# Flamingo-style gated decoder, layer 1 attention: the finishing of a unit is issued between the maxima and the scores of its batch

## The reference, cut to what matters

```python
xn = (x - mu) * jax.lax.rsqrt(var + EPS) * ln_g + ln_b
q = _split_heads(xn @ Wq)
kv = xn @ Wkv
k = _split_heads(kv[..., :INNER])
v = _split_heads(kv[..., INNER:])
mem = _split_heads(memories @ Wm)
k = jnp.concatenate([k, mem], axis=2)
v = jnp.concatenate([v, mem], axis=2)
scale = DIM_HEAD ** (-0.5)
dots = jnp.einsum('bhid,bhjd->bhij', q, k) * scale
attn = jax.nn.softmax(dots, axis=-1)
out = jnp.einsum('bhij,bhjd->bhid', attn, v)
...
return out @ Wo + bo
```

## Time and profile before

| | us |
|---|---|
| median of 3 runs | 5704.32 |
| lowest and highest | 5701.73, 5706.47 |
| profiled execution | 5706.84 |
| its span (first to last instruction of the program) | 5705.1 |
| units of layer 1 attention in it | about 442 to 2883 |

### The profile page before, as it was taken

One profiled execution on the slowest core, in us unless ns is written; L12 is line 12 of the kernel. 1 busy time (PEld: TensorE's weight loads), 2 busy tenths in 40 slices (PEclk: granted clock), 3 DMA queues, 4 the chain that ended last, 5 costly groups with the idle time before them and its releaser, 6 DMA issues. The chain is left out here.

```text
span 5705.1 us, 74603 instructions
## 1 busy us (share of the span) xinstructions
PE 5058.3 (89%) x26863; PEld 1958.8 (34%) x26872; DVE 4773.0 (84%) x5111; ACT 3066.1 (54%) x5929; POOL 1556.1 (27%) x1168
## 2 busy tenths in 40 slices
PE   8939999999999999999932799999997599999997
PEld 5524444445454544444411222222223122222222
DVE  7459989898989899899868899999982799999993
ACT  3314444444444444444410288888882188888884
POOL 0015556565656565655612000000000200000000
PEclk9969999999999999999965799999995599999996
DMA  0043233333324232322102211111100411111100
GB/s 30 1 131 101 65 94 86 91 87 85 104 67 122 55 115 53 105 70 55 28 4 61 47 21 21 26 21 21 26 7 7 100 21 21 25 22 21 21 16 5
DMA packets 164054, 293.78 MB, mean 51 GB/s; under 512 B 26492, under 2 KB 103752, under 8 KB 160616
## 3 DMA queue, kind: packets, MB, share of 16 engines
q1 hardware_dynamic: 159592, 287.70, 20.4%
q10 hardware_dynamic: 4096, 1.29, 0.1%
HBM read 178.92 MB, written 109.89 MB: 51 GB/s over the span
## 5 line engine op out<-in xcount | busy, mean ns | idle before, releaser
L1599 DVE TENSOR_REDUCE a_mx<-ps 128x1 f32<-128x1024 f32 x1536 | 1820.2, 1220 | 151.4 <-PE ps L1479 129.4
L1566 ACT ACTIVATE a_prob<-ps 128x512 f32<-128x512 f32 (+1 forms) x3264 | 1705.3, 601 | 426.9 <-PE ps L1467 422.2
L1060 ACT ACTIVATE prob<-ps 128x512 f32<-128x512 f32 (+1 forms) x1888 | 975.0, 602 | 1181.9 <-PE ps L945 1181.8
L1163 POOL TENSOR_TENSOR tot_p<-tot_p,prob 128x512 f32<-128x512 f32 (+1 forms) x896 | 1340.4, 1496 | 921.6 <-ACT prob L1060 856.6
L1088 DVE TENSOR_REDUCE mx<-ps 128x1 f32<-128x1024 f32 x896 | 1051.3, 1215 | 152.9 <-PE ps L922 145.1
L1111 DVE TENSOR_TENSOR tot_d<-tot_d,prob 128x512 f32<-128x512 f32 x928 | 1047.8, 1129 | 87.6 <-ACT prob L1060 36.2
L1479 PE MATMUL ps<-a_K,a_Q 51*128 51x512 bf16 (+1 forms) x3328 | 1068.3, 385 | 49.6 <-DMA a_Q<-q_stack_dram 30.3
L1467 PE MATMUL ps<-a_Q,a_K 51*128 51x512 bf16 (+1 forms) x3264 | 1003.8, 389 | 82.8 <-ACT a_prob L1566 76.6
L1503 PE MATMUL ps<-a_prob,a_V 128*9 128x512 f32 x6528 | 953.9, 609 | 10.9 <-ACT a_acc L1550 10.9
L956 PE MATMUL ps<-prob,V 128*64 128x512 f32 (+1 forms) x3776 | 934.0, 605 | 0.0
L944 PE MATMUL ps<-QA,KA 128*128 128x512 f32 (+1 forms) x1888 | 806.4, 427 | 0.0
(11 more groups left out here) (348 smaller groups left out, 3243.4 us busy)
## 6 DMA issues: line engine op xcount, KB each, us to landing
a_K<-k_stack_dram SPq DMA_DIRECT2D x64, 600.4 KB, 5.8
k_hi_dram<-hi_s SPq DMA_DIRECT2D x112, 256.0 KB, 2.0
k_lo_dram<-lo_s SPq DMA_DIRECT2D x112, 256.0 KB, 2.0
KA<-k_hi_dram SPq DMA_DIRECT2D x64, 384.0 KB, 4.3
KA<-k_lo_dram SPq DMA_DIRECT2D x64, 384.0 KB, 5.5
KB<-k_hi_dram SPq DMA_DIRECT2D x64, 384.0 KB, 6.5
k_bf_dram<-bf_s SPq DMA_DIRECT2D x112, 128.0 KB, 1.7
KM<-k_bf_dram SPq DMA_DIRECT2D x32, 448.0 KB, 7.1
```

The costliest lines, as they stand in the source:

```text
L1060: nc.scalar.activation(prob[0:r, batch % 2, t % BATCH, :], c.banks(n % 3)[0:r, :], ACT.Exp, scale=SCALE).then_inc(exped, 1)
L1163: nc.gpsimd.tensor_tensor(tot_p[0:r, u % 2, :], tot_p[0:r, u % 2, :], p, ALU.add).then_inc(totalled_p, 1)
L1566: nc.scalar.activation(prob[0:r, batch % 2, t % BATCH, :], c.banks(n % 3)[0:r, :], ACT.Exp, scale=SCALE).then_inc(exped, 1)
L1599: nc.vector.tensor_reduce(mx[:, u % 2, j, i % FULL:i % FULL + 1], c.banks(slot(step), 2), AX.X, ALU.max).then_inc(maxed, 1)
```

## The change

In the loop over the batches the finishing is issued earlier on two engines. On PE it now stands between the maxima and the scores of batch 1; before, it stood between the scores and the weighing. On DVE it now stands between the two reductions of maxima and the two row sums of batch 1; before, it stood behind the row sums. The numbers of the slots, the waits, the instructions themselves, and the order on ACT, POOL and SP are the same. It applies to 31 of the 32 finishings; the one behind the last batch stays where it is.

```diff
@@ PE
                         for step in max_steps(u, b):
                             max_score(*step)
+                        kind, what = extra_of(u, b) or (None, None)
+                        if kind == "fin":
+                            finish(what)
                         for t in tiles_of(b):
                             score(u, t)
-                        kind, what = extra_of(u, b) or (None, None)
                         if kind == "k":
                             project(what)
                         if kind == "v":
                             project_v(*what)
-                        if kind == "fin":
-                            finish(what)
```

## The result

The changed kernel takes 5779.76 us (median of 4, 5772.55 to 5788.25) against 5703.49 before: a ratio of 1.013, 95% interval 1.0117 to 1.0143. It is 76 us slower. The forecast was slower as well, but by 48 us, and its range ended at 5770. The profiled execution took 5779.97 us, with a span of 5777.1.

The account below looks back on a forecast made before the run. The prediction took PE to set the pace, with DVE trailing and PE stopping only at finishings. Order +20.6 us and clock +27 us, about 48 in all, on 5704.3 gave 5752 us, range 5719 to 5770.

Parts of the forecast that it names:

- What bounds the kernel: Layer 1's units: PE sets the pace and stops only at finishings, 23 times, 28.4 us in all, waiting for DVE.
- DVE's lag costs nothing: Time from PE's first maximum of batch 1 to DVE's start on it, 0.44 to 1.32 us, had not cost PE anything.
- DVE is the bound after all: Rival: DVE's queue delays the units, so the 28.4 us of stops are gained and the new wait covered; 5676 us, chance 0.03.
- DVE's lag shrinks: Rival: DVE reaches batch 1 only 0.43 us behind PE in all units, clock up; 5712 us, chance 0.05.
- The stop removed, the stop added: On PE: 28.4 us at batch 2's second maximum go; the finishing waits for its batch's first reduction, about 46 us in all.
- The order's cost: PE's new order without any clock effect, summed over three kinds of unit and unit 31: +20.6 us.
- The number of falls: PE's granted clock drops at three of four of the new stops: 23 falls, bounds 0 and 30.
- The last finishing of the kernel before: Sign: behind the last batch PE idles 0.88 us, then runs the finishing, and the granted clock falls to 0.55.
- What one fall costs: PE's clock lowered for 3.4 us, read from layer 0: 1.2 us lost, bounds 0 and 1.54; +27 us in all.
- its dearest case: Rival: PE's clock falls at every place and at full price, 20.6 + 46 = 67 us; 5771 us, chance 0.07.
- the clock holds: Rival: PE's clock stays up at the new stops, so only +20.6 us counts; 5725 us, chance 0.23.

Follow-up runs that it names:

- DVE's half alone: Kernel before with only DVE's finishing moved ahead of its two row sums, PE's order unchanged: 5695.51 us, ratio 0.998.
- the kernel with the stop filled: Changed kernel plus six score matmuls that do no useful work ahead of each finishing on PE: 5726.55 us, ratio 1.0036.
- PE's half alone: Kernel before with only PE's finishing moved between maxima and scores, DVE's order unchanged: 5785.1 us, ratio 1.0142.
- the kernel with the wait apart: Changed kernel with PE's wait kept between maxima and scores, the finishing's matmuls put back behind the scores: 5781.87 us; run again, 5756.74 us.
- the version with the split row sums: Kernel before with DVE's finishing moved between its two row sums of batch 1, PE's order unchanged: 5672.63 us, ratio 0.9944.

## Why the prediction was wrong, point by point

**What bounds the kernel.** Right on PE and on the stops. The claim that DVE's lag costs nothing was true of the kernel before and held in the changed one, but it had less room than I gave it: in the kernel with DVE's half alone, 1.26 us of idle time on DVE was enough to give back 23 of 34 us. The rival "DVE is the bound after all" was therefore wrong about this change and half right about the kernel. DVE's row sums did get shorter, 0.69 us each in unit 2 in place of 3.38 for both, and PE had no use for that time. "DVE's lag shrinks" did not come true: in unit 2 it stayed at 0.80, and in unit 3 it went only from 1.32 to 1.09.

**The stop removed, the stop added.** Right. 28.4 us gone, 47.1 added at 30 places (forecast about 46), up to 2.0 us long (2.1). The order's cost came out at 17.5 us against 20.6, and the kernel with the stop filled lies 20.5 us above the kernel before. Each kind was 0.05 to 0.2 us cheaper than its sum, partly because the reduction releases its slot a little earlier than 1.36 us after its start (1.31 to 1.32 in units 2 and 12), and in unit 3 because the lag was 1.09 and no longer 1.32.

**The number of falls.** 23 in units 1 to 30, as taken. That the number agrees to the unit is luck: "three of four" was chosen between 0 and 30, and PE's half alone fell at 28 of nearly the same 30 stops. The last finishing of the kernel before had pointed to the falls, and the reason that I gave, idle time beside the sparse finishing, is part of it (the kernel with the finishing behind the weighing). It is not all of it: the kernel with the wait apart fell 13 and 15 times. Length and neighbours both count. The trace of before had a second sign that I passed over: the fall at 74.3 came within a microsecond of two stops of 1.03 and 1.20 us with two matmuls of 128 columns between them, so stops of that length were not safe as such.

**What one fall costs.** This is the step that failed. I took 3.4 us of low clock for each, read from one fall in layer 0, and 1.2 us of loss, because I held the finishing to be paced by its many instructions. Both were too low. The stretch in layer 0 showed the short form only; half of the falls here last 6.8 us. The longer form was there to be read: the trace of before has the granted clock at 0.50 for 6.8 us near its start, from 23.1 to 29.9. And the finishing does slow down: in unit 2 its last matmuls take 0.77 us instead of 0.47. A low stretch costs 1.56 / 3.4 = 0.46 us per microsecond in this kernel, and 3.15 / 6.8 is the same, so a short fall costs the full price of 1.54 that I had as the upper bound. The mean over the 24 falls is 56.5 / 24 = 2.35 us, and even my upper bound for a fall was below it. 23 x (2.35 - 1.2) = 26 us is nearly the whole miss of 28; the fall in unit 31, which the sum did not have, adds 1.6, and the order came out 3 us cheaper.

**The range.** It ended at 5770 since its dearest case was 30 falls at 1.54 us. A bound on a price that was read from one example was no bound. The last finishing of the kernel before could not have told the length either, as PE has nothing to do behind it.

**The rival "the clock holds".** It did not: the clock fell after stops of 0.88 to 2.04 us, between other work. The Trainium skill, "TensorE: Matmul & The Clock Gate", section "HAM oscillation — how this bites in real kernels", warns only of longer idle gaps. The measurement decides against reading that as a safe limit.

## What to carry to other kernels

A slot that rotates ties a step to the step two before it: moving a step closer to that one turns hidden time into a wait, even if the other wait goes. Before a stop is put on PE, look at what PE does right before and after it; a stop of one to two microseconds beside sparse matmuls can cost more by the clock than by its length, and a filled stop tells the two apart in one run. Where an engine waits for the result of another in the middle of its queue, put one of its own independent instructions there, as the version with the split row sums does.

## What the runs showed of the hardware

The granted clock fell after stops of 0.88 to 3.28 us on PE. How often depended on length and neighbours. Between weighing, maxima and scores, 23 stops of 1.1 to 1.3 us never lowered it, and neither did 14 of 1.15 (two traces); of 28 stops of 1.51 us there 13 did, and of 18 of 1.80 us 15. With the finishing close ahead 13 of 30 stops of 1.2 us did, with the finishing right behind, in the changed kernel, 4 of 7 of 1.15, 10 of 14 of 1.51 and all 9 longer ones did, and all 30 when the stop was 1.1 us longer still. In units 1 to 31 a low stretch lasted 3.4 or 6.8 us, and PE work in it did not end it earlier; near the end of unit 31's work, in the last finishing, one of 106 us begins in both kernels. Where falls come at some places only, the spread between the four runs of a kernel was 9 to 26 us, with 16 in the changed kernel. It was 4 where every place falls, and 3 to 9 in the kernels whose traces show no fall in the units, over 3 to 14 runs.
